# Attention heads: chunks of turned scores dealt out anew, two counts of the 256-column tile on VectorE, ranks compared for two tiles at a time

## The reference, cut to what matters

```python
draft = jnp.einsum('bhqd,bhkd->bhqk', qr, kr)
draft = draft + jnp.where(causal_future, neg, jnp.asarray(0.0, dtype))
num_remain = max(min(Sq, MIN_REMAIN), Sq - int(Sq * MASK_OUT))   # 128
_, draft_indices = jax.lax.top_k(draft, num_remain)
mask = jnp.full((B, H, Sq, Sq), neg, dtype)
mask = mask.at[b_idx, h_idx, s_idx, draft_indices].set(0.0)
mask = jnp.where(causal_future[None, None, :, :], neg, mask)
scores = jnp.einsum('bhqd,bhkd->bhqk', qr, kr) / np.sqrt(HD).astype(np.float32) + mask
attn = jax.nn.softmax(scores, axis=-1)
out = jnp.einsum('bhqk,bhkd->bhqd', attn, v)
```

## Time and profile before

| | before |
|---|---|
| median of 3 runs | 3198.43 us (3196.75 to 3200.32) |
| the profiled execution | 3197.66 us, span 3195.9 us |
| TensorE busy | 2783.8 us (87%) |
| VectorE busy | 2479.8 us (78%) |
| ScalarE busy | 1957.4 us (61%) |
| GpSimd busy | 1650.3 us (52%) |
| turns of the head loop | from about 2060 to 3070 us |

### The profile page before, as it was taken

One profiled execution on the slowest core, in us unless ns is written; L12 is line 12 of the kernel. 1 busy time (PEld: TensorE's weight loads), 2 busy tenths in 40 slices (PEclk: granted clock), 3 DMA queues, 4 the chain that ended last, 5 costly groups with the idle time before them and its releaser, 6 DMA issues. The chain is left out here.

```text
span 3195.9 us, 50444 instructions
## 1 busy us (share of the span) xinstructions
PE 2783.8 (87%) x15722; PEld 1538.3 (48%) x15833; DVE 2479.8 (78%) x4664; ACT 1957.4 (61%) x4186; POOL 1650.3 (52%) x3659
## 2 busy tenths in 40 slices
PE   8899999999999999999999989747777777777669
PEld 4455455454464554554554544514444444444444
DVE  6677687696696786876976976759888888888746
ACT  2464554564554545545645523579999999999723
POOL 3236245263263362452542644777777777777503
PEclk9999999999999999999999999859889888988989
DMA  2222222132132231221321310000000000000010
GB/s 95 59 80 93 73 99 80 66 116 89 59 113 78 71 110 66 88 91 66 103 76 60 119 48 27 1 1 2 2 2 2 2 2 2 2 2 2 2 50 27
DMA packets 65804, 169.62 MB, mean 53 GB/s; under 512 B 11776, under 2 KB 19328, under 8 KB 64512
## 3 DMA queue, kind: packets, MB, share of 16 engines
q1 hardware_dynamic: 54448, 115.17, 11.1%
q10 hardware_dynamic: 11088, 51.19, 4.6%
HBM read 161.08 MB, written 5.24 MB: 52 GB/s over the span
## 5 line engine op out<-in xcount | busy, mean ns | idle before, releaser
L2088 ACT ACTIVATE X<-ah_z,ah_trial 128x256 bf16<-128x256 f32 (+6 forms) x896 | 731.6, 822 | 27.0 <-POOL ah_trial L2189 16.5
L1207 ACT ACTIVATE m_mix<-m_mix,m_cs 128x128 f32<-128x128 f32 x1024 | 312.9, 388 | 252.0 <-DMA m_mix<-cs_rows 252.0
L1089 POOL TENSOR_TENSOR m_xdec<-m_xdt,m_decay_out 128x512 f32<-128x512 f32 x112 | 143.2, 1279 | 213.2 <-DVE m_xdt L1333 202.1
L1117 POOL TENSOR_TENSOR m_squares<-m_squares 128x256 f32<-128x256 f32 x128 | 104.6, 817 | 275.9 <-ACT m_squares L1219 275.9
L2099 ACT ACTIVATE X<-ah_ps_e 128x512 f32<-128x512 f32 (+3 forms) x384 | 184.2, 480 | 86.6 <-PE ah_ps_e L2009 53.9
L1013 PE MATMUL m_ps_d<-m_w_out,m_gate 128*128 128x512 f32 x512 | 235.2, 602 | 0.0
L1013 PE MATMUL m_ps_x<-m_w_out,m_gate 128*128 128x512 f32 x512 | 233.7, 599 | 0.0
L2279 DVE MAX8 ah_top<-ah_ps_m 128x8 f32<-128x256 f32 (+6 forms) x224 | 186.2, 831 | 54.8 <-PE ah_ps_m L1973 50.4
L2258 DVE TENSOR_SCALAR_CACHE_REDUCE X<-ah_z,ah_cut 128x256 bf16<-128x256 f32 (+6 forms) x224 | 193.6, 875 | 38.2 <-POOL ah_cut L2194 38.2
L2249 DVE TENSOR_SCALAR_CACHE_REDUCE ah_z<-ah_ps_z 128x256 f32<-128x256 f32 (+6 forms) x224 | 182.6, 816 | 13.9 <-PE ah_ps_z L1952 13.9
L2181 POOL TENSOR_TENSOR ah_slope<-ah_between,ah_table 128x7 f32<-128x7 f32 x128 | 193.4, 1511 | 0.0
(11 more groups left out here) (326 smaller groups left out, 7611.4 us busy)
## 6 DMA issues: line engine op xcount, KB each, us to landing
m_mix<-cs_rows SPq DMA_DIRECT2D x128, 512.0 KB, 4.4
m_w_proj<-in_w_proj ACTq DMA_DIRECT2D x69, 512.0 KB, 3.3
m_fade<-fade_rows SPq DMA_DIRECT2D x224, 128.0 KB, 2.9
m_w_out<-in_w_out ACTq DMA_DIRECT2D x7, 2048.0 KB, 8.0
X<-in_x SPq DMA_DIRECT2D x8, 256.0 KB, 4.8
m_w_out<-in_w_out SPq DMA_DIRECT2D x1, 2048.0 KB, 9.9
x_away<-X SPq DMA_DIRECT2D x1, 2048.0 KB, 7.3
X<-x_away SPq DMA_DIRECT2D x8, 256.0 KB, 6.1
```

The costliest lines, as they stand in the source:

```text
L1207: act.activation(mix[:, u % 3, h, :], mix[:, u % 3, h, :], ACT.Relu, bias=cs[:, c, h0 + h:h0 + h + 1], scale=-1.0).then_inc(lag_done, 1)
L2088: act.activation(sign[:, at % 2, 0:(t + 1) * P], z[:, h % RING, cols(t)], ACT.Sign, bias=trial[:, h % RING, 0, t - 1:t], scale=-1.0, accum ...
```

## The change

Three edits, all in `attention_heads_fast`.

First, the chunks of turned scores are dealt out anew over TensorE's order of a turn: chunk 2 now stands with chunk 1 at the start, ahead of the marked scores of tile 1, chunk 3 takes its place, and later chunks move one or two places forward.

Second, the counts k = 0 and k = 2 of tile 1 (256 columns) are made by VectorE (`count_low`), which counts scores below the trial and starts from -128. GpSimd doubles that into the place of ScalarE's sum. ScalarE's sweeps with k = 0 and k = 2 begin at tile 2. The copy of the output (`keep_out`) moves on VectorE from before the two first takes to behind them.

Third, the ranks are compared with the counts for two tiles in one operation, between the maximum and the predicated copy of tiles 1, 3 and 5 (one tile alone at 7), where before each tile had its own.

```diff
-    CHUNKS_FIRST = (1,)
-    CHUNKS_AFTER_MARKED = ((), (), (), (), (), (7,), (9,), ())
-    CHUNKS_AFTER_SCORES = ((), (2,), (3, 4), (5,), (6,), (8,), (10,), (11,))
+    CHUNKS_FIRST = (1, 2)
+    CHUNKS_AFTER_MARKED = ((), (), (), (), (6,), (), (), (11,))
+    CHUNKS_AFTER_SCORES = ((), (3,), (4,), (5,), (7,), (8, 9), (10,), ())
...
+    ON_VECTOR = ((0, 0), (1, 2))
+    scalar_tiles = lambda k: range(2 if k in [q for _, q in ON_VECTOR] else 1, NT)
+    SCALAR_AT = {hkt: i for i, hkt in enumerate((h, k, t) for h, k in order for t in scalar_tiles(k))}
+    VECTOR_AT = {hk: i for i, hk in enumerate(hk for hk in order if hk[1] in [q for _, q in ON_VECTOR])}
...
+        lower = sb("lower", [P, RING])
+        below = sb("below", [P, 2 * P], BF16)
-        surplus = sb("surplus", [P, 2, 8], I32)
+        surplus = sb("surplus", [P, W, 8], I32)
...
         def _(act):
             def count(h, k, t):
-                if t == 1 and k == 0:
-                    act.wait_ge(guessed, h + 1)
-                elif t == 1:
-                    act.wait_ge(moved, MOVE_AT[h, k - 1] + 1)
+                if t == scalar_tiles(k)[0]:
+                    if k == 0:
+                        act.wait_ge(guessed, h + 1)
+                    else:
+                        act.wait_ge(moved, MOVE_AT[h, k - 1] + 1)
                 if k == 0:
                     act.wait_ge(z_done, h * NT + t + 1)
-                at = MOVE_AT[h, k] * W + t - 1
+                at = SCALAR_AT[h, k, t]
                 if at >= 2:
                     act.wait_ge(counted, at - 1)
                 act.activation(sign[:, at % 2, 0:(t + 1) * P], z[:, h % RING, cols(t)], ACT.Sign,
...
-                        if live(n - back):
+                        if live(n - back) and t in scalar_tiles(k):
...
-                pool.wait_ge(counted, (MOVE_AT[h, k] + 1) * W)
+                if (h, k) in VECTOR_AT:
+                    pool.wait_ge(counted_low, VECTOR_AT[h, k] + 1)
+                    pool.tensor_scalar(signs[:, r, 0:1], lower[:, r:r + 1], 2.0, None, ALU.mult).then_inc(own, 1)
+                    at += 1
+                    pool.wait_ge(own, at)
+                pool.wait_ge(counted, SCALAR_AT[h, k, NT - 1] + 1)
...
             def excess(h, t):
-                at = h * W + t - 1
-                if at >= 2:
-                    dve.wait_ge(pick_step, 3 * at - 3)
-                dve.wait_ge(take_done, at + 1)
-                dve.tensor_scalar(surplus[:, at % 2], ranks[:], taken_count[:, h, t - 1:t], float(TOPK), ALU.add,
-                                  ALU.is_ge).then_inc(pick_step, 1)
+                to = min(t + 2, NT)
+                if h:
+                    dve.wait_ge(pick_step, 2 * h * W)
+                dve.wait_ge(take_done, h * W + to - 1)
+                dve.tensor_tensor(surplus[:, t - 1:to - 1], taken_count[:, h, t - 1:to - 1].unsqueeze(2).to_broadcast([P, to - t, 8]),
+                                  ranks[:].unsqueeze(1).to_broadcast([P, to - t, 8]), ALU.is_ge).then_inc(excess_done, 1)
+
+            def count_low(h, k):
+
+                at = VECTOR_AT[h, k]
+                if k == 0:
+                    dve.wait_ge(guessed, h + 1)
+                    dve.wait_ge(z_done, h * NT + 2)
+                else:
+                    dve.wait_ge(moved, MOVE_AT[h, k - 1] + 1)
+                if at:
+                    dve.wait_ge(counted_low, at)
+                dve.tensor_scalar(below[:], z[:, h % RING, cols(1)], trial[:, h % RING, 0, 0:1], -float(P), ALU.is_lt, ALU.add,
+                                  accum_out=lower[:, h % RING:h % RING + 1]).then_inc(counted_low, 1)
             def pick(h, t):
...
                 r = at % 2
                 if at >= 2:
                     dve.wait_ge(pick_done, at - 1)
-                if t == 1:
-                    excess(h, t)
                 dve.wait_ge(marked, at + 1)
                 dve.max(top[:, r], ps_m[:, m_at(t):m_at(t) + (t + 1) * P]).then_inc(pick_step, 1)
-                dve.wait_ge(pick_step, 3 * at + 2)
-                dve.copy_predicated(top[:, r], surplus[:, r], taken8[:]).then_inc(pick_step, 1)
-                if t < W:
-                    excess(h, t + 1)
+                if t % 2:
+                    excess(h, t)
+                dve.wait_ge(excess_done, h * (NT // 2) + (t + 1) // 2)
+                dve.wait_ge(pick_step, 2 * at + 1)
+                dve.copy_predicated(top[:, r], surplus[:, t - 1], taken8[:]).then_inc(pick_step, 1)
                 if h >= 2:
                     dve.wait_ge(et_done, (h - 2) * NCH + LAST_CHUNK[t] + 1)
-                dve.wait_ge(pick_step, 3 * at + 3)
+                dve.wait_ge(pick_step, 2 * at + 2)
                 dve.match_replace(picked[:, h % 2, cols(t)], top[:, r], ps_m[:, m_at(t):m_at(t) + (t + 1) * P],
                                   TAKEN).then_inc(pick_done, 1)
...
                     evacuate(n + 1, 0)
                     sample(n + 1)
                     add_sample(n + 1)
-                if live(n - 4):
-                    keep_out(n - 4)
+                if live(n - 1):
+                    count_low(n - 1, 2)
                 if live(n - 2):
                     take(n - 2, 1)
                     take(n - 2, 2)
+                if live(n - 4):
+                    keep_out(n - 4)
                 for t in range(1, NT):
+                    if t == 4 and live(n + 1):
+                        count_low(n + 1, 0)
                     if live(n - 2):
                         pick(n - 2, t)
                     if live(n + 1):
...
-            "cut_table": cut_table.astype(np.float32), "ranks8": np.arange(8, dtype=np.float32),
+            "cut_table": cut_table.astype(np.float32), "ranks8": TOPK - np.arange(8, dtype=np.float32),
```

More of the change, by code:

```diff
@@ L1904, in attention_heads_fast @@
             sem("s_done"), sem("z_done"), sem("sampled"), sem("stats_done"), sem("guessed"))
-        counted, moved, cut_done, own = sem("counted"), sem("moved"), sem("cut_done"), sem("own")
+        counted, counted_low, excess_done = sem("counted"), sem("counted_low"), sem("excess_done")
+        moved, cut_done, own = sem("moved"), sem("cut_done"), sem("own")
         take_done, marked, pick_step, pick_done, least_done = (
```

## The result

The changed kernel took 3214.79 us (median of 5 runs, 3213.24 to 3216.51) against 3196.75 us of the kernel before in the same session: a ratio of 1.0053, 95% interval 1.004 to 1.0066. It is 18 us slower. The forecast was 3222 us, in a range of 3191 to 3237.

What follows compares the result with a forecast made beforehand. The head loop was taken as bound almost equally by cycles through GpSimd and VectorE. VectorE's terms summed to +1.16, taken as +0.85 us a turn; 28 turns give 24 us, so 3222 us, range 3191 to 3237.

Steps and rivals of the forecast that it cites:

- Two cycles have nearly this length: In the head loop, cycles of waits through GpSimd (29.50 us) and through VectorE (29.62 us) bind almost equally.
- Part 1: Two counts leaving ScalarE (0.98 us a turn) and chunk 2 turned earlier both lie beside GpSimd's chain: gain 0.
- GpSimd cycle: From one third sweep of ScalarE to the next, through GpSimd's cut, first guess and move: 29.5 us, 29.3 after the change.
- Part 2: One scaling added in each of two GpSimd moves: +0.31 us on its cycle, with 0.55 of chunk waits gone.
- Part 3: VectorE gets two counts at +0.41 us each; the first covers its 0.27 us wait for the cut.
- Part 4: On VectorE, removed comparisons save nothing; new ones between maximum and copy cost +0.15 us each, +0.45 for three.
- Part 5: Output copied after both takes, so chunk 0's product delays the first marked scores: take 1 to first maximum 0.89 becomes 2.37 us.
- I expect it to stay: TensorE's clock, from before the first marked scores to after the second, stays at 0.50, the level of 1.2 GHz.
- a clock above 0.9 there: Sign that the forecast is wrong: TensorE's granted clock above 0.9 at the first marked scores, where 0.50 was expected.
- The rival "no change": TensorE keeps 2.4 GHz across the boundary, so VectorE's cycle grows by 0: 3198 us, chance 0.12.
- The rival "faster": VectorE's cycle does not grow, GpSimd's 29.3 us binds, chunk 7's wait is gained: -0.25 a turn, 3191 us, chance 0.12.

Runs made afterwards that it cites:

- number 4: The changed kernel with the copy of the output back ahead of the takes; 3191.69 us, ratio 0.9983 to the kernel before.
- number 6: The kernel before with only GpSimd's first guess of the next head moved behind the second move; 3195.64 us, ratio 0.9993.
- number 10: The kernel before with chunk 2 ahead of the first marked scores and chunks 3 and 4 moved up behind it; 3179.83 us, ratio 0.9939.
- number 9: The kernel before with only chunks 6, 7, 9 and 11 dealt forward; 3180.69 us, ratio 0.995.
- number 2: The kernel before with only the two counts of tile 1 on VectorE and GpSimd's doubling; 3210.31 us, ratio 1.004.
- number 11: The changed kernel with GpSimd's first guess moved behind the second move; 3379.7 us, ratio 1.0572 to the kernel before.
- number 3: The kernel before with only the comparison of ranks for two tiles in one operation; 3203.2 us, ratio 1.0017.
- number 7: The kernel before with only the copy of the output moved behind both takes; 3220.14 us, ratio 1.007.
- the best version: The kernel before with the new dealing of chunks and GpSimd's first guess moved behind the second move; 3153.51 us, ratio 0.9857.

## Why the prediction was right, and where it was not

Direction and range were right, and the size was close: +25 forecast, +18 measured. That closeness is in part luck. In the turn the forecast was +0.85 and the runs show +0.48, and some 4 of the 18 us lie outside the 27 turns, where the forecast had one more turn of 0.85 and nothing else. The sum was better than its terms. From the experiments the terms are, in us a turn: dealing -0.65, counts +0.43, comparisons +0.07, late copy +0.70 in the changed kernel; together +0.55 against +0.48 measured. In times, -22.4 + 12.7 + 5.6 + 23.1 = +19. The last term is the difference between the changed kernel and number 4, so what this sum tests is the first three: -4.1 us against the -5.9 of number 4.

- **"Two cycles have nearly this length"** was the reading that failed in part. The turn of 29.5 us was right for both, but neither bound alone: the first guess off GpSimd's chain gained nothing (number 6). The sign taken for GpSimd's cycle, a third sweep 0.25 us behind the move, was ScalarE's own work, and the earlier trace rows had it: all 77 counts of 256 columns waited 0.8 us in sum for the trial. The cycle through chunk 2 was not seen. It was visible in the rows that the forecast used: ScalarE waited 18.8 us for chunk 2, and TensorE turned chunk 2 only after it had waited for take 1.
- **Part 1, "The same holds for chunk 2 ... so 0"** is the step that was wrong by most: chunk 2 forward alone is worth 0.63 us a turn (number 10). The later chunks alone are worth 0.70 (number 9), where 0.55 stood, and only on the GpSimd cycle. The reason given, that sweep two lies beside the GpSimd chain, held only while the GpSimd chain was the longer one.
- **Part 1, the two counts off ScalarE at 0**: the direction holds. Counts alone made the kernel slower (number 2).
- **Part 2**: the doubling costs its queue 0.33 us (from 2610.03 to 2610.36 in the changed kernel's GpSimd timeline) as forecast at 0.31. Where the GpSimd cycle binds, that is what it costs: 0.33 in number 4, whose usual turn of 29.2 us is nearly the 29.3 that the forecast gave this cycle. The 14 short turns of the changed kernel have this length too. What the kernel would gain without the doubling no run shows; number 11 was to tell and could not.
- **Part 3**: a count takes 473 ns and 0.40 of queue; forecast 0.41. Averaged over 26 turns of VectorE's timeline, tile 3's to tile 4's replacement grew from 3.37 to 3.84 us. Right.
- **Part 4**: copy to value load is 0.28 us, as before and as said, so the removed comparisons gained nothing. The copy stands 0.12 us behind the end of the maximum (2578.56 against 2578.44), 0.09 later than before, where 0.15 was taken: the new comparison lasts 159 ns, not 0.23 us. The advice of the Trainium skill, "VectorE: DVE Perf Modes", section "Rules for kernel authors", to minimise the count of operations brought nothing in this place (number 3, ratio 1.0017): what went had filled a delay.
- **Part 5**: the term is real and the largest, 0.70 us a turn. Its mechanism was half of the matter. The product of chunk 0 is one reader of the copy, and the turning of the output is another; number 7 shows that the second alone suffices in the kernel before. How the 0.70 divides between the two in the changed kernel was not run. The size by its own steps was off too: first maximum +0.36 us (2.75 to 3.11 over 26 turns) where the calculation with 1.2 GHz gave +0.73 beside the reduction, and from the first maximum to the second tile's replacement -0.95 where -0.43 stood, because the clock was mostly not low there. In the 7 of 26 turns where it was, the first maximum stood up to 3.5 us behind the reduction, as the calculation had it (3.4).
- **"I expect it to stay"**, of the clock's fall at the boundary: wrong, and this is one of the forecast's own signs of being wrong ("a clock above 0.9 there", which 19 of 26 turns had). The mean granted clock in 2300 to 2867 rose from 0.89 to 0.92. A fall came instead at tile 7, in 18 of 27 turns, where it took 0.43 us a turn (14.5 / 19 us of wait against 6.2 / 19 before). The Trainium skill, "TensorE: Matmul & The Clock Gate", section "HAM oscillation — how this bites in real kernels", says that gaps bring the clock down and that work packed together keeps it up. The traces agree: the falls follow TensorE's gap, now the one of up to 2.5 us before tile 7, and number 10, where chunk 2 alone is packed into the boundary, has fewer of them and no new place.

The rival "no change" had the clock at the boundary right in most turns and was wrong in the end; it did not count the fall's new place. The rival "faster" asked the GpSimd cycle to bind, which it did with the dealing and without the late copy: number 4 took 3191.69 us, where the rival stood at 3191. The late copy is what kept it from being right.

## What to carry to other kernels

In a loop of engines in lockstep, list every cycle, above all those that pass through the in-order queue of an engine that is not the bound: a transfer or product waits not only for its data but for all that its queue has ahead. Where two engines show small waits for each other all the time, no share of busy time names the bound; shorten one suspected cycle by an edit that touches no other, and see if the turn moves. An edit that makes an engine do less work gains nothing while it waits, and an edit that gives work to an engine whose queue others wait for costs even if that engine has idle time.

When a copy is moved later, look for all its readers and at what stands behind each of them: 36 us hung on one reader's place. And an aid that reads an early value (the low count, which needs the guess) ties down the producer of that value; here it closes the way to the best version, with the guess in the place tried.

## What the runs showed that was not expected

- A dependent operation on VectorE starts 0.03 to 0.12 us behind the recorded end of the one it needs, an independent one about 0.08 ahead of it. An operation put into that gap is free, and taking it out gains nothing: copy to load is 0.28 us with it and without.
- TensorE's fall to 1.2 GHz goes with the gaps, though TensorE's work in a turn was the same. Chunk 2 put into the gap at the boundary took falls away (26 to 15 in 27 turns) and brought none elsewhere. The later chunks taken from before tile 7 widened the gap there from 1.42 to as much as 2.40 us, and the clock then fell there in 15 of 27 turns (number 9).
- A mean turn can hide two kinds. The changed kernel's 30.02 us are 14 turns of 29.2, the GpSimd cycle with the doubling in it, and 13 turns of 30.9.
- Edits of one cycle are not additive (18 and 19 us, together 22). The parts of the change came close to it (19 against 18); no run shows a reason, and with cycles this near to each other it may be chance.
